# Taking the first layer's first three runs side by side in a four-layer GNN stack on one core

## Time and profile before

| what | value |
|---|---|
| time, median of 3 runs | 1113.02 us (1112.81 to 1114.36) |
| the profiled execution | 1112.82 us |
| its span in the trace | 1111.0 us |
| PE busy | 1094.4 us, 99% of the span |
| DVE busy | 1045.5 us, 94% |
| ACT busy | 918.9 us, 83% |
| POOL busy | 57.4 us, 5% |
| DMA | 408.35 MB, mean 368 GB/s |
| granted TensorE clock | 0.999 |

### The profile page before, as it was taken

How to read it: one execution, slowest core, us unless ns; L and a number is a source line. 1 busy time by engine, 2 the same in 40 slices (tenths; PEclk the granted TensorE clock), 3 DMA queues, 4 the chain that set the end, 5 groups by cost and what they waited for, 6 DMA issues and landing times.

```text
span 1111.0 us, 14659 instructions
## 1 busy us (share of the span) xinstructions
PE 1094.4 (99%) x4992; PEld 908.3 (82%) x4992; DVE 1045.5 (94%) x1443; ACT 918.9 (83%) x1304; POOL 57.4 (5%) x46
## 2 busy tenths in 40 slices
PE   6999999999999999999999999999999999999998
PEld 5888888888888888888888888888887877878886
DVE  7899998999999999989989899999989999999997
ACT  7899998798788688888787788888888988887774
POOL 2000000000000000000000021121111121110000
PEclk9999999999999999999999999999999999999999
DMA  9999999999998999999999999999999999999992
GB/s 344 409 409 407 403 399 359 355 397 409 364 373 310 357 409 409 409 390 356 353 377 399 373 348 361 368 353 372 359 383 329 389 349 344 378 371 401 354 366 107
DMA packets 113834, 408.35 MB, mean 368 GB/s; under 512 B 12640, under 2 KB 13920, under 8 KB 113760
## 3 DMA queue, kind: packets, MB, share of 16 engines
q1 hardware_dynamic: 113760, 407.42, 96.7%
HBM read 405.27 MB, written 2.10 MB: 367 GB/s over the span
## 4 chain that ended last, share of the span: by engine, by line
PE 83%; DVE 14%; ACT 1%; issue 1%; POOL 1%; DMA 1%; SPq 0%; ACTq 0%
PE bank L800 53%; PE bank L804 27%; DVE a_lo L551 11%; PE bank L821 3%; DVE stats L609 1%; DMA raw<-in_adj_t_dram 1%; DVE x_sb L699 0%; DVE zt L690 0%; DVE h_lo L602 0%; POOL std L392 0%; PE bank L811 0%; DVE raw L545 0%; ACT a_hi L412 0%; DVE mv L613 0%; POOL act_raw L378 0%
## 5 line engine op out<-in xcount | busy, mean ns | idle before, releaser
L551 DVE TENSOR_TENSOR a_lo<-raw,a_hi 128x1024 fp32r<-128x1024 f32 x560 | 657.4, 1218 | 31.9 <-ACT a_hi L410 14.0
L800 PE MATMUL bank<-a_hi,h_hi 128*128 128x512 f32 x1400 | 436.5, 393 | 9.0 <-ACT a_hi L412 9.0
L410 ACT ACTIVATE a_hi<-raw 128x1024 fp32r<-128x1024 f32 x368 | 379.4, 1056 | 73.3 <-PE bank L804 64.9
L804 PE MATMUL bank<-a_lo,h_hi 128*128 128x512 f32 x1400 | 433.3, 391 | 3.3 <-DVE a_lo L551 3.2
L800 PE MATMUL bank<-a_hi,h_lo 128*128 128x512 f32 x1400 | 432.2, 390 | 0.0
L804 PEld LDWEIGHTS bank<-a_lo,h_hi 128*128 128x128 f32 x1400 | 262.2, 188 | 62.4 <-DVE a_lo L551 8.1
L800 PEld LDWEIGHTS bank<-a_hi,h_hi 128*128 128x128 f32 x1400 | 260.0, 188 | 60.6 <-issue 9.0
L800 PEld LDWEIGHTS bank<-a_hi,h_lo 128*128 128x128 f32 x1400 | 263.4, 188 | 55.4
L412 ACT ACTIVATE a_hi<-raw 128x1024 fp32r<-128x1024 f32 x192 | 201.8, 1054 | 23.3 <-PE bank L804 10.4
L551 DVE TENSOR_TENSOR a_lo<-acc,a_hi 128x1024 fp32r<-128x1024 f32 x144 | 170.7, 1217 | 6.0 <-ACT a_hi L410 4.4
L410 ACT ACTIVATE a_hi<-acc 128x1024 fp32r<-128x1024 f32 x144 | 147.6, 1059 | 24.6 <-PE bank L804 23.4
(11 more groups left out here) (77 smaller groups left out, 410.8 us busy)
## 6 DMA issues: line engine op xcount, KB each, us to landing
raw<-in_adj_t_dram SPq DMA_DIRECT2D x496, 512.0 KB, 6.7
acc<-in_adj_t_dram SPq DMA_DIRECT2D x144, 512.0 KB, 6.2
raw<-in_adj_dram SPq DMA_DIRECT2D x128, 512.0 KB, 7.9
out_dram<-x_sb SPq DMA_DIRECT2D x7, 256.0 KB, 5.1
x_sb<-in_x_dram SPq DMA_DIRECT2D x3, 512.0 KB, 9.1
x_sb<-in_x_dram SPq DMA_DIRECT2D x2, 256.0 KB, 3.1
out_dram<-x_sb SPq DMA_DIRECT2D x2, 128.0 KB, 1.7
w_sb<-in_L_gnn_W_dram SPq DMA_DIRECT2D x3, 64.0 KB, 9.0
```

The costliest lines, as they stand in the source:

```text
L410: act.activation(sub_hi_of(n), sub_raw(n), ACT.Copy).then_inc(sub_hi, 1)
L551: dve.tensor_tensor(sub_lo_of(n), sub_raw(n), sub_hi_of(n).bitcast(F32), ALU.subtract).then_inc(sub_lo, 1)
L800: pe.matmul(bank[half][:, :], weights, hi_a[:, half * GW:(half + 1) * GW], start=start and weights is hi_w, stop=False)
L804: last = pe.matmul(bank[half][:, :], hi_w, lo_a[:, half * GW:(half + 1) * GW], start=False, stop=stop)
```

## The change

Four things are changed, all in the first layer's part with b = 0.

1. The order of steps 0 to 23. A constant SIDE = 4 is added: steps 0 to 11 take feature blocks 0, 1, 2, 3 and for each of them the three runs 0, 1 and 2 in turn (run 0 in banks 0 and 1, run 1 in banks 2 and 3, run 2 in banks 4 and 5). Then runs 0, 1 and 2 take their blocks 4 to 7 one run at a time, and end at steps 15, 19 and 23. From step 24 on the order is as before.
2. The loading of x. In front of the first tile come blocks 0 and 1 alone (128 KB); blocks 2 to 7 (384 KB) are issued behind the third tile.
3. The pieces of the first layernorm are (0,2), (2,4), (4,8), then as before. Piece 0 still goes over DVE and ACT. GpSimd no longer takes part: pieces 1 and 2 are normalized by ACT (L440) as the later ones are, with statistics on DVE behind steps 2 and 6, the square root behind 3 and 8, the bias on DVE behind 3 and 8, the relu on ACT behind 4 and 9, and the low part on DVE behind 4 and 10.
4. The places of DRAIN. For b = 0 the banks are emptied at the last step plus 5 (and 6) instead of plus 7 (and 8); for the other b nothing changes. That holds for all eight runs with b = 0: the copies of run 7 move from behind hi(118) and hi(119) to behind hi(116) and hi(117).

The core of the diff:

```diff
@@ -125,15 +125,20 @@
+        SIDE = 4
         runs = []
...
         run_end = []
+        for i in range(SIDE):
+            seq += [(d - 1, 0, d, i, i == 0, False) for d in range(1, NG)]
         for b in range(NG):
...
                     runs.append((kind, d, b))
-                    seq += [(len(runs) - 1, kind, d, b * CB + i, i == 0, i == CB - 1) for i in range(CB)]
+                    done = SIDE if (kind, b) == (0, 0) else 0
+                    seq += [(len(runs) - 1, kind, d, b * CB + i, i == 0, i == CB - 1) for i in range(done, CB)]
                     run_end.append(len(seq) - 1)
@@ -224,12 +229,7 @@
-        NORMED = 4
-        FIRST = [(b, b + GB // 2) for b in range(0, CB, GB // 2)] + [(GB * q, GB * q + GB) for q in range(2, NQ)]
-        def chain_n(i):
-            return i if i < 3 else i - 1
+        FIRST = [(0, 2), (2, GB)] + [(GB * q, GB * q + GB) for q in range(1, NQ)]
@@ -276,7 +276,7 @@
-        DRAIN = {run_end[r] + 7 - 3 * (runs[r][2] >= 2) + half: (r, half) for r in range(len(runs)) for half in range(2)}
+        DRAIN = {run_end[r] + (5, 7, 4, 4)[runs[r][2]] + half: (r, half) for r in range(len(runs)) for half in range(2)}
@@ -300,12 +300,11 @@
...
-        FIRST_STATS = {24: 4, 36: 5, 50: 6, 64: 7, 77: 8, 90: 9}
-        FIRST_STD = {28: 4, 40: 5, 54: 6, 68: 7, 81: 8, 94: 9}
-        FIRST_AFFINE = {29: 4, 41: 5, 55: 6, 69: 7, 82: 8, 95: 9}
-        FIRST_RELU = {32: 4, 44: 5, 58: 6, 71: 7, 84: 8, 97: 9}
-        FIRST_HI = {0: 1, 2: 2, 3: 3}
-        FIRST_LO = {0: 1, 2: 2, 3: 3, 33: 4, 45: 5, 59: 6, 72: 7, 85: 8, 98: 9}
+        FIRST_STATS = {2: 1, 6: 2, 24: 3, 36: 4, 50: 5, 64: 6, 77: 7, 90: 8}
+        FIRST_STD = {3: 1, 8: 2, 28: 3, 40: 4, 54: 5, 68: 6, 81: 7, 94: 8}
+        FIRST_AFFINE = {3: 1, 8: 2, 29: 3, 41: 4, 55: 5, 69: 6, 82: 7, 95: 8}
+        FIRST_RELU = {4: 1, 9: 2, 32: 3, 44: 4, 58: 5, 71: 6, 84: 7, 97: 8}
+        FIRST_LO = {4: 1, 10: 2, 33: 3, 45: 4, 59: 5, 72: 6, 85: 7, 98: 8}
@@ -324,7 +323,7 @@
...
             def load_x(i):
-                b0, b1 = (0, GB) if i == 0 else (GB, CB) if i == 1 else ((i - 1) * CB, i * CB)
+                b0, b1 = FIRST[0] if i == 0 else (FIRST[1][0], CB) if i == 1 else ((i - 1) * CB, i * CB)
                 sp.dma_start(x_sb[:, b0:b1, :], x[:, b0:b1, :]).then_inc(x_in[i], 16)
@@ -337,9 +336,10 @@
...
             load_x(0)
-            load_x(1)
             for n in range(RAWS):
                 load(n)
+                if n == 2:
+                    load_x(1)
             weights = (w_in, w_out, w1, w2, w3)
@@ -372,19 +372,6 @@
...
-            def first_norm(i):
-                b0, b1 = FIRST[i]
-                for n in range(b0, b1):
-                    last = pool.tensor_scalar(act_raw[:, n % GB * D:(n % GB + 1) * D], x_sb[:, n, :], mv0[:, n, 0:1],
-                                             rstd0[:, n:n + 1], ALU.subtract, ALU.mult)
-                last.then_inc(act_ready, 1)
-            for i in range(1, NORMED):
-                pool.wait_ge(rstd0_ready, chain_n(i) + 1)
-                if i > 1:
-                    pool.wait_ge(h_ready, i - 1)
-                first_norm(i)
@@ -412,8 +399,8 @@
...
             def first_std(i):
-                blocks = slice(FIRST[i][0], FIRST[3 if i == 2 else i][1])
-                act.wait_ge(mv0_ready, chain_n(i) + 1)
+                blocks = slice(*FIRST[i])
+                act.wait_ge(mv0_ready, i + 1)
                 act.activation(std0[:, blocks], mv0[:, blocks, 1], ACT.Sqrt, bias=eps_sb[:, 0:1]).then_inc(std0_ready, 1)
@@ -427,14 +414,9 @@
...
-            def first_hi(i):
-                b0, b1 = FIRST[i]
-                act.wait_ge(act_ready, i + 1)
-                act.activation(h_hi[0][:, b0:b1, :], act_blocks(b0, b1), ACT.Relu).then_inc(h_hi_ready, 1)
...
                 b0, b1 = FIRST[i]
-                act.wait_ge(bias0_ready, i - NORMED + 1)
+                act.wait_ge(bias0_ready, i)
                 act.wait_ge(h_ready, i)
@@ -485,8 +467,6 @@
...
                     first_std(FIRST_STD[n])
-                if n in FIRST_HI:
-                    first_hi(FIRST_HI[n])
                 if n in FIRST_RELU:
@@ -500,13 +480,11 @@
...
             first_std(0)
-            first_hi(0)
-            first_std(1)
+            act.wait_ge(act_ready, 1)
+            act.activation(h_hi[0][:, 0:2, :], act_blocks(0, 2), ACT.Relu).then_inc(h_hi_ready, 1)
             for n in range(S0):
...
                 hi(n, deg_part[:, 1 - kind, k, d:d + 1])
-                if n == 0:
-                    first_std(2)
                 first_layer(n)
@@ -550,45 +528,33 @@
...
-            def first_bn(b0, b1):
-                for b in range(b0, b1):
+            def first_stats(i):
+                blocks = range(*FIRST[i])
+                dve.wait_ge(x_in[0 if i == 0 else FIRST[i][0] // CB + 1], 16)
+                for b in blocks:
                     last = dve.bn_stats(stats0[:, b, :], x_sb[:, b, :])
-                return last
-            def first_aggr(i, b0, b1):
-                dve.wait_ge(stats0_ready, chain_n(i) + 1)
-                for b in range(b0, b1):
+                last.then_inc(stats0_ready, 1)
+                dve.wait_ge(stats0_ready, i + 1)
+                for b in blocks:
                     last = dve.bn_aggr(mv0[:, b, :], stats0[:, b, :])
...
-            def first_stats(i):
-                b0, b1 = FIRST[i]
-                dve.wait_ge(x_in[b0 // CB + 1], 16)
-                first_bn(b0, b1).then_inc(stats0_ready, 1)
-                first_aggr(i, b0, b1)
-            def first_rstd(i, b0, b1):
-                dve.wait_ge(std0_ready, chain_n(i) + 1)
-                dve.reciprocal(rstd0[:, b0:b1], std0[:, b0:b1]).then_inc(rstd0_ready, 1)
+            def first_rstd(i):
+                blocks = slice(*FIRST[i])
+                dve.wait_ge(std0_ready, i + 1)
+                dve.reciprocal(rstd0[:, blocks], std0[:, blocks]).then_inc(rstd0_ready, 1)
+                dve.wait_ge(rstd0_ready, i + 1)
...
                 blocks = slice(*FIRST[i])
-                first_rstd(i, *FIRST[i])
-                dve.wait_ge(rstd0_ready, chain_n(i) + 1)
+                first_rstd(i)
                 dve.scalar_tensor_tensor(out=bias0[:, blocks], in0=mv0[:, blocks, 0], scalar=-1.0, in1=rstd0[:, blocks],
...
-            def first_norm(i):
-                b0, b1 = FIRST[i]
-                for n in range(b0, b1):
-                    last = dve.tensor_scalar(act_raw[:, n % GB * D:(n % GB + 1) * D], x_sb[:, n, :], mv0[:, n, 0:1],
-                                             rstd0[:, n:n + 1], ALU.subtract, ALU.mult)
-                last.then_inc(act_ready, 1)
...
                 dve.wait_ge(h_hi_ready, i + 1)
-                if i < NORMED:
+                if i == 0:
                     dve.scalar_tensor_tensor(out=h_lo[0][:, b0:b1, :], in0=act_blocks(b0, b1), scalar=0.0,
@@ -737,24 +703,15 @@
...
-            dve.wait_ge(x_in[0], 16)
-            first_bn(0, 2).then_inc(stats0_ready, 1)
-            first_aggr(0, 0, 2)
-            first_bn(2, 4).then_inc(stats0_ready, 1)
-            first_rstd(0, 0, 2)
-            dve.wait_ge(rstd0_ready, 1)
-            first_norm(0)
-            first_aggr(1, 2, 4)
-            dve.wait_ge(x_in[1], 16)
-            first_bn(4, 6)
-            first_rstd(1, 2, 4)
+            first_stats(0)
+            first_rstd(0)
+            for n in range(2):
+                last = dve.tensor_scalar(act_raw[:, n * D:(n + 1) * D], x_sb[:, n, :], mv0[:, n, 0:1],
+                                         rstd0[:, n:n + 1], ALU.subtract, ALU.mult)
+            last.then_inc(act_ready, 1)
             first_lo(0)
-            first_bn(6, 8).then_inc(stats0_ready, 1)
-            first_aggr(2, 4, 8)
             for n in range(S0):
                 lo(n)
-                if n == 0:
-                    first_rstd(2, 4, 8)
                 first_layer(n)
```

## The result

The changed kernel took 1115.95 us (median of 13 runs, 1114.61 to 1117.55), the kernel before, run beside it, 1112.75 (13 runs, 1112.30 to 1114.36). The ratio is 1.0027, with a 95% interval of 1.0020 to 1.0034: 3.2 us slower, where 3.6 were forecast. The profiled execution took 1117.55 us, with a span of 1115.8, against 1112.82 and 1111.0.

A forecast was written before the change was run, and what follows sets the result against it. PE was taken as the bound, 99% busy and without a gap from 64 to 365 us, so lateness carries to the end. Terms +1.36 and +2.25 make +3.6 on the median 1113.02: 1116.5 us, range 1114.0 to 1118.3.

The forecast's parts named there:

- PE's start: Step 0: with 384 KB less ahead of tile 0, PE starts at 7.8 instead of 9.02, 1.2 us earlier.
- The chain to step 12: From tile 3 on, ACT and DVE work in turn, so PE begins step 12 near 30.6 instead of 28.55.
- the dear one: ACT's wait near 22.3 for the bias of piece 2, with all later high parts behind it; 1.3 us.
- The first term: Late start: PE reaches step 38 at 65.96 instead of 64.60, +1.36 us; bounds 0 and +2.5.
- The tight place at step 37: Norm of blocks 8 to 11 makes step 37's low part end at PE's heels; moved copies end it 0.5 us sooner.
- The second term: Run 7's earlier copies put DVE two low parts behind, PE late by step 153: +2.25 us; bounds 0 and 2.3.
- The sum: Whole kernel: 1.36 + 2.25 = +3.6 us, said as 1116.5; both terms together had chance 0.60.
- The first: Rival: only the start is late, run 7's copies do no harm; +1.36, 1114.4 us; chance 0.10.
- second: Rival: only the drain is late, PE is level at step 38; +2.25, 1115.3 us; chance 0.17.
- The third: Rival: PE falls to the slow pace in new waits between steps 5 and 11; 1119.2 us; chance 0.08.
- The fourth: Rival: not slower, lo(11) ends before 27.7, gain capped at 0.5 us by step 37; 1112.5 us; chance 0.05.
- the list of signs: Timeline signs: ACT idles 0.4 us near 15, 1.3 near 22.3; PE's low part waits rise from 3.2 to over 7.

The follow-up runs named there:

- e3: The changed kernel with both pieces of x loaded ahead of the first tile, as in the kernel before; 1114.36 us, ratio 1.0008.
- e1: The changed kernel with only run 7's two copies put back to plus 7 and 8; 1113.53 us, ratio 1.0003.
- e8: The changed kernel with the third sweep's layernorm scale one low part later (PASS_AFFINE 3: 12 instead of 11); 1117.82 us, ratio 1.0033.
- e4: The changed kernel with relu and low part of piece 2 put behind step 11 instead of 9 and 10; 1113.55 us, ratio 1.0004.
- e7: The changed kernel with only DVE's reciprocal and bias of piece 2 behind step 7 instead of 8; 1116.08 us, ratio 1.0017.
- e2: The kernel before with only run 7's two copies moved from plus 7 and 8 to plus 5 and 6; 1114.09 us, ratio 1.0012.
- e10: The kernel before with, in the third sweep behind a norm's statistics, DVE's next low part ahead of the identity addition; 1111.32 us, ratio 0.9987.
- e9: e5 with, in the third sweep behind a norm's statistics, DVE's next low part ahead of the identity addition; 1111.32 us, ratio 0.9986.
- e5: The changed kernel with relu and low part of piece 2 behind step 11, and run 7's copies at plus 7 and 8; 1113.84 us, ratio 1.0002.
- e6: e5 with the copies of all kind 1 runs (3, 4, 5 and 7) at plus 7 and 8; 1113.85 us.

## Why the prediction was right, point by point

**PE's start.** 6.49 instead of 7.8: tile 0 was there at 5.20. The start moved by 2.5 us where I took 1.2, but not for the bytes alone: e3 has all of x in front and starts at 7.36, so the bytes are worth 0.9. The other 1.7 came with x in pieces of 128 and 384 KB instead of two of 256, or with something else of the change; no run here separates that. It is also no fixed size, since the kernel before started at 9.02, 9.95 and 9.85 us in its three profiles. In the first microseconds the DMA moves far less than the 412 GB/s of the earlier trace rows: between 2 and 8 us 281 GB/s in the profile before and 259 in the one after. It did not matter: e3 shows that step 12 does not follow the start.

**The chain to step 12.** hi(3) began at 12.52 (12.4 forecast), the relu of piece 2 at 23.76 (23.63), hi(10) at 25.98 (25.84), the low part of step 11 at 30.16 (30.04). Steps 12 and 38 came 0.13 us behind the forecast, and the links between by 0.12 to 0.17: the error is the landing of tile 3. In e1 and e8 tile 3 came at 12.15 and 12.22 and step 12 at 30.36 and 30.43, each time 18.21 us behind, as here. e4 and e7 show that the wait for the bias is the dear one.

**The first term** was +1.36, and is 1.13 at step 115 (171.49 to 172.62). At step 38 it was 1.49. The rest had been lost by the kernel before anyway: its PE met DVE's low parts once more at steps 99 and 100, 0.24 us, and with 1.5 us of lateness the new one did not. I had said that PE has no gap between 64 and 365 us; delays of a tenth are too small for the list of waits and show only in the spacing of the matmuls.

That the first term came out so close is in part luck with the profile. The forecast took 28.55 for step 12 of the kernel before, and 0.7 us lost from there to step 38. In e2 and e10, with the same code up to there, step 12 begins 0.9 us later, nothing is lost behind it, and the low part of step 115 comes at 171.38 and 171.29, even a little sooner than at 171.49. The profile before had an early start and then a late tile:

```profile
37.44 1.06 ACT L412 ACTIVATE a_hi<-raw 128x1024 fp32r<-128x1024 f32 x1 [0.97 <-DMA raw<-in_adj_t_dram]
```

It is high part 21, which began at 36.74 in e2. The tight place at step 37 is thus not the work of the norm alone, as I had read the earlier trace rows, but also of this tile: lo(37) started at 62.77 there and at 62.01 in e2. Over three profiles of either kernel, the first term is 0.9 to 1.5 us at step 38 and 0.8 to 1.3 at step 115. One more step of the working was wrong: lo(37) ends at 63.89 in the changed kernel and not at 63.5, so moving the copies did not bring it sooner. That cost nothing, since PE came later still.

**The second term** was +2.25, and is 2.24: 3.37 at step 153 less 1.13. Of that, 1.38 had come by step 127, as forecast. e1 and e2 show it by itself in either kernel.

**The sum** was 3.6, and is 3.37 at step 153. Medians: 3.2. The profiled executions differ by 4.7, of which 1.4 is a second long GpSimd operation.

**The rivals.** The first and second each had one term; both are there. The third, a return to the slow pace: step 8, with the banks in turn, has its pairs of matmuls 0.46 us apart (22.94, 23.41, 23.87), as later, and in step 11, behind the wait of 1.29 us in front of step 10, they are again 0.46 apart (28.99, 29.45). By these rows the rule of the Trainium skill (TensorE: Matmul & The Clock Gate, the section on psum-queue depth-cycling) does not take hold here. The fourth would have needed lo(11) to end before 27.7; e4 does that (PE takes it at 27.58). Its cap of 0.5 us at step 37 was wrong, since e4 is 1.1 us ahead at step 38; but such a lead is lost again: by step 115 e4 is only 0.5 to 0.7 us ahead, and e9 not at all.

**What was wrong in the list of signs**: ACT idled for the bias by 0.28 us near 15 and 1.19 near 22.5, where 0.4 and 1.3 were forecast. PE's waits for low parts rose from 3.2 to 5.2 us, not above 7. I had counted delays that the list puts down to high parts, and small ones that it leaves out.

## What to carry to other kernels

A wait has its price from what is queued behind it on its engine. Here the norm's bias was needed only for step 12, but ACT waited for it in front of the high parts of steps 10 and 11; two places later it cost nothing. And where a copy waits for another engine's fixed step, moving it earlier in its own queue doesn't bring it sooner, it only puts more work behind the wait. An earlier first instruction is worth something only if the chain that sets a later step starts sooner too: look for that chain first. And a single profile can hold two accidents that cancel, here an early start and a late tile; a second profile of the same code shows it.

## What the runs showed of the hardware

The executions of one kernel lie in heaps, and part of that comes from a near coincidence of two instructions. In the third sweep GpSimd adds eps to four variances (L392, L379 after). It takes 1.09 us in most places. Where it starts 0.01 to 0.02 us before a DVE low part (two inputs in SBUF), which happens twice in each of the ten profiles without the edit of e9, it takes 1.29 us (ten times) or 3.96 (eight times; 5.30 both times in e8). From the kernel before, around 847 and 909 us:

```profile
847.38 3.96 POOL L392 TENSOR_TENSOR std<-mv,eps_sb 128x4 f32<-128x4 f32 x1 [17.45 <-DVE mv L613]
847.39 1.22 DVE L551 TENSOR_TENSOR a_lo<-acc,a_hi 128x1024 fp32r<-128x1024 f32 x1
...
850.06 1.22 DVE L551 TENSOR_TENSOR a_lo<-raw,a_hi 128x1024 fp32r<-128x1024 f32 x1
...
909.65 1.29 POOL L392 TENSOR_TENSOR std<-mv,eps_sb 128x4 f32<-128x4 f32 x1 [17.85 <-DVE mv L613]
909.66 1.22 DVE L551 TENSOR_TENSOR a_lo<-acc,a_hi 128x1024 fp32r<-128x1024 f32 x1
```

The long one ends at 851.34, when DVE has ended its run of low parts (851.28) and waits, and e8 lengthened it to 5.30 by lengthening the run. The short ones end in the same way: all 192 of these additions, in twelve profiles, end 0.05 to 0.06 us behind the end of a DVE instruction. That holds for those of 1.09 us too, which start when DVE's low part is 0.16 us under way (in e9 the low part ends at 848.19 and GpSimd at 848.25), and for those of 1.29, which are longer by what they start earlier against the low part. So 1.09 is the time until DVE lets go, by these rows, and not a time undisturbed beside DVE. What sets the long one apart is that it does not get in at the end of the first DVE instruction, nor at the next three, but at that of the last before DVE stands. The Trainium skill (SBUF — State Buffer, the section on the two separate sides) describes the port pair that the two engines share as an exclusive lock, which goes to whoever starts first for the whole instruction, and which also DVE operations with two SBUF inputs take against a GpSimd read. The trace agrees in so far as GpSimd is held up to the end of a DVE instruction. It differs in two ways: by the recorded starts GpSimd was first, by 0.01 to 0.02 us, and was held all the same, and a long one stays out over several instructions in a row. Why one such start is let in and the next is not, no run here shows. In e1 to e4, measured on one chip, all eight were short; in e5 to e8, on another, seven of eight were long.

What it costs can be read from the time between the low part of step 153 and the end of the span: 883.8 to 884.0 us in the profiles without one of 3.96 (e1 to e4, e9, e10), 885.1 and 885.2 with one (before, e7), 886.5 with two (after, e5, e6). So 1.2 to 1.4 us each. The eleven times of e1 lie in three heaps, 1112.4 to 1112.6, 1113.5, and 1114.9 to 1115.1, about as far apart; that they stand for none, one and two long ones is not shown, since only the first has a profile. Other scatter is left: e9 and e10 spread over 1.5 and 1.6 us, and e5's profile with two long ones is among its fastest. In a study of 2 us, all that is as much as the change itself; the positions of the same step in two traces tell more than two medians, and several traces more than two.
